# A Macaron block (MoE, state-space mixer, MoE): on GpSimd's queue, the third group's scatter goes ahead of the first group's gather

## The reference

```python
x = L0_attn_x                                    # 4 x 1024 tokens, 256 wide
x = x + 0.5 * ffn(layernorm(x))                  # block 1
x = x + attn(layernorm(x))                       # in_proj, conv, state-space scan, gate, norm, out_proj
x = x + 0.5 * ffn(layernorm(x))                  # block 2, same weights
# ffn: every token goes through 2 shared experts and 4 of 16 routed ones
tidx, tw = _route(x, router_weight, e_bias)      # best 2 of 4 groups, then the 4 best experts
h = silu(x @ gate.T) * (x @ up.T);  y = h @ down.T
routed = sum over the 4 chosen of tw * y;  out = routed + shared
```

## Time and profile before

| what | value |
|---|---|
| time, median of 3 runs | 1771.51 us (1762.28 to 1775.17) |
| the profiled execution's own time | 1766.28 us |
| its span, first to last instruction | 1764.5 us |
| mean granted TensorE clock | 0.911 |
| PE busy | 1460.1 us (83%) |
| DVE, ACT, POOL busy | 1038.3, 702.0, 997.7 us |

### The profile page before, as it was taken

One profiled execution on the slowest core, in us unless ns is written; L12 is line 12 of the kernel. 1 busy time (PEld: TensorE's weight loads), 2 busy tenths in 40 slices (PEclk: granted clock), 3 DMA queues, 4 the chain that ended last, 5 costly groups with the idle time before them and its releaser, 6 DMA issues. The chain is left out here.

```text
span 1764.5 us, 24364 instructions
## 1 busy us (share of the span) xinstructions
PE 1460.1 (83%) x7430; PEld 1218.3 (69%) x7430; DVE 1038.3 (59%) x2279; ACT 702.0 (40%) x1191; POOL 997.7 (57%) x982
## 2 busy tenths in 40 slices
PE   5889989999704689999999998997588989999970
PEld 4678878888603467777777776776577878888860
DVE  5544255335534487888888788886655425533543
ACT  4244434444204444454544444443323433444420
POOL 2706735537464776675767667574170773554746
PEclk9999989999956599999999989999699999999995
DMA  9826456757334000010000100000623645675733
GB/s 377 347 106 229 151 170 219 267 182 261 118 124 139 0 1 12 25 37 13 25 13 24 36 11 25 12 24 12 257 93 106 235 144 172 234 259 179 258 110 122
DMA packets 91286, 226.25 MB, mean 128 GB/s; under 512 B 16673, under 2 KB 29985, under 8 KB 90273
## 3 DMA queue, kind: packets, MB, share of 16 engines
q1 hardware_dynamic: 66592, 157.68, 25.1%
q0 software_dynamic: 24576, 67.14, 11.6%
HBM read 115.72 MB, written 109.05 MB: 127 GB/s over the span
## 5 line engine op out<-in xcount | busy, mean ns | idle before, releaser
L746 PE MATMUL f_gu_ps<-f_wgu,f_xT 128*128 (+1 forms) x1920 | 470.6, 390 | 0.0
L369 POOL DMA_INDIRECT f_gbuf<-yg,f_rows x256 | 261.9, 1023 | 261.0 <-DVE f_xin L617 121.7
L746 PEld LDWEIGHTS f_gu_ps<-f_wgu,f_xT 128*128 128x128 f32 x1920 | 357.5, 196 | 41.1
L345 POOL DMA_INDIRECT xg<-f_xn,f_rows x256 | 251.5, 982 | 210.0 <-DVE f_rows L560 133.9
L596 DVE TENSOR_TENSOR f_h<-f_gu_ps,f_sg 128x256 f32<-128x256 f32 x240 | 101.4, 423 | 349.3 <-ACT f_sg L413 348.3
L767 PE MATMUL f_y_ps<-f_wd,f_hT 128*128 (+1 forms) x960 | 248.1, 387 | 29.1 <-DVE f_hT L602 29.0
L767 PEld LDWEIGHTS f_y_ps<-f_wd,f_hT 128*128 128x128 f32 x960 | 183.0, 193 | 62.2 <-DVE f_hT L602 23.2
L1383 DVE SCALAR_TENSOR_TENSOR at_xs<-at_raw,at_taps,at_xs 128x512 f32<-128x512 f32 x144 | 188.7, 1310 | 29.9 <-POOL at_xs L1122 27.4
L413 ACT ACTIVATE f_sg<-f_gu_ps 128x256 f32<-128x256 f32 x240 | 91.8, 384 | 283.2 <-PE f_gu_ps L746 282.9
L396 ACT COPY f_xT<-f_xT_ps 128x512 f32<-128x512 f32 x224 | 131.4, 587 | 146.0 <-PE f_xT_ps L722 134.9
L617 DVE SCALAR_TENSOR_TENSOR f_xin<-f_gbuf,f_w,f_xin 128x256 f32<-128x256 f32 x256 | 123.7, 485 | 78.6 <-DMA f_gbuf<-yg,f_rows 71.7
(11 more groups left out here) (224 smaller groups left out, 2611.7 us busy)
## 6 DMA issues: line engine op xcount, KB each, us to landing
f_xq<-xg SPq DMA_DIRECT2D x88, 512.0 KB, 4.5
yg<-f_yo SPq DMA_DIRECT2D x176, 256.0 KB, 2.7
xg<-f_gbuf SPq DMA_DIRECT2D x32, 512.0 KB, 17.4
f_wgu<-in_gate_up SPq DMA_DIRECT2D x4, 1280.0 KB, 21.3
at_x_ln<-x SPq DMA_DIRECT2D x10, 512.0 KB, 3.9
f_xin<-in_x SPq DMA_DIRECT2D x8, 512.0 KB, 6.9
xg<-f_xn,f_rows POOLq DMA_INDIRECT x256, 3.7
f_gbuf<-yg,f_rows POOLq DMA_INDIRECT x256, 3.4
```

Source lines behind the costliest of these rows:

```text
L345: G.indirect_dma_start(xg[g], bass.IndirectOffsetOnAxis(ap=rows[g][:, b, k:k + 1], axis=0), xn[:, SUB * TILE0[g] + b, :], None, bounds_che ...
L369: G.indirect_dma_start(gbuf[:, n % GBUF, k, :], None, yg[g], bass.IndirectOffsetOnAxis(ap=rows[g][:, b, k:k + 1], axis=0), bounds_check=2 ...
L746: last = T.matmul(gu_ps[:, j % 2, s * 2 * P:(s + 1) * 2 * P], x_of(k, s, d), weight(wgu[:, :, d, :], experts[s]), start=(d == 0), stop=(d ...
```

## The change

```diff
             rstd_of(t)
         scatter_group(0)
         scatter_group(1)
+        scatter_group(2)
         gather_group(0)
-        scatter_group(2)
         gather_group(1)
         gather_group(2)
```

## The result

The changed kernel took 1846.14 us (median of 4, 1844.93 to 1847.92) against 1773.34 us (median of 4): ratio 1.042, 95% interval 1.0369 to 1.0471. Forecast was 1847 us, slower. The profiled execution took 1847.92 us, and its span is 1846.2 us.

The account below looks back on a forecast made before the run. TensorE (PE) was taken to set the time in the stage touched. Two blocks of 36.0 us stall plus 3.1 restart, no gain, made 78.2 us on 1768.8: 1847 us, range 1832 to 1862.

Parts of the forecast that it names:

- (a): GpSimd's queue, block 1: after waiting 41 us for the addresses, the first moved scatter starts at 262.55 us.
- (b): GpSimd's queue, block 1: 32 scatters at 1.28 us take 41.0 us, so the first gather starts at 303.5.
- Step (c): Group 0's first gather to its combination: 7.24 us (9.23 the upper end), so DVE stands 38.0 us.
- Step (d): PE at L767, block 1: resumes 2.85 us after DVE's combination starts, at 313.6, and loses 36.0 us.
- Step (e): PE's first round after the stall: restart at a lowered clock costs 3.1 us more, making 39.1 a block.
- The sum: Both FFN blocks: 2 x 39.1 = 78.2 us on a mean of 1768.8, giving 1847 us, 4.4% slower.
- rival 2: Third group's start: existing stalls there, 11 us in all, take back part of the loss; 1834 to 1845 us, chance 0.15.
- No gain on the other side: Third group's scatter: its first reader, load L275 at 351.16, has 7 us of spare, so the gain is 0.
- Rival 1: Group 0's gathers land slowly or later combinations wait too: 2 to 9 us more a block, 1851 to 1865, chance 0.15.
- one sign of being wrong: Third group's start: the prediction called itself wrong if the stalls there shrink; no size given.
- Rivals 3 and 4: No change if addresses were ready by 223.7 us (1769 us, chance 0.02); faster through an earlier scatter (1748 us, chance 0.02).
- The rule on the shared port: Moved scatters: would go faster while DVE stands; rule and rows differ by a few tenths of a us a block.

Follow-up runs that it names:

- e1: Kernel before, with GpSimd waiting for the third group's addresses ahead of group 0's gathers, scatters still behind: 1767.85 us, ratio 0.9981.
- e4: Kernel before, with only 16 of the third group's 32 scatters moved ahead of group 0's gathers: 1807.61 us, ratio 1.0198.
- e2: Kernel before, with the new order in the first FFN block alone: 1811.77 us, ratio 1.0224.
- e3: Kernel before, with the third group's scatter placed between group 0's first four and last four gathered blocks: 1800.61 us, ratio 1.0169.
- e9: Changed kernel, with group 0's first combination in event 16 in place of 10: 1811.30 us, ratio 1.0196 to the kernel before.
- e5: Changed kernel, with group 0's combinations from event 22 on in place of 10: 1771.24 us, ratio 0.9971 to the kernel before.
- e6: Kernel before, with the second group's combinations one event (3.25 us) later: 1768.66 us, ratio 0.9957.
- e7: Kernel before, with the second group's combinations two events later, the last ones packed: 1762.38 us, ratio 0.9912.

## Why the prediction was right

**Steps (a) and (b), the date of the first gather.** Forecast 262.55 and 303.5; measured 261.58 and 302.46. Both are 1.0 earlier, because the addresses were: L560 stands at 260.61 in place of 261.58. The second group began no earlier (its first transposition at 225.87, against 225.81), but the granted clock in the 5 us from 225 on was 0.62 in place of 0.50. From that transposition to L560 the eleven kernels take 34.7 to 36.4 us, least where the clock is highest and without regard to GpSimd's order, so nothing puts this 1.0 us down to the change. The 40.9 us between the two dates are as forecast, and 32 scatters at 1.28 us each were the heart of it. e1 and e4 show that this is the right cause: the wait alone costs nothing, and each scatter is worth 1.27 us of DVE's wait.

**Step (c), gather to combination.** Forecast 7.24, measured 6.99 in block 1 and 7.01 in block 2 (1581.49 to 1588.50). The choice of 7.24 over 9.23 was right, but the reason given wasn't: the row called quiet was not. The DMA share from 377.25 to 384.49 was 0.70, against 0.73 in the 9.23 us of block 2, and PE was busy through all of the 7.24. In the stall, at 0.31, the same step took only 0.25 us less. What makes block 2's second group slower (9.23, and 8.55 in the changed kernel) stays open.

**Step (d), PE's loss.** DVE's wait forecast 38.0, measured 37.58 and 37.57; PE resumed 2.85 us after the combination's start in both. PE's 36.0 were 35.48 and 35.47 by its own row.

**Step (e), the restart.** Forecast 3.1, measured 5.93 - 3.25 = 2.68 and 6.39 - 3.25 = 3.14. The other waits of 10.1 us or more, in e2, e3, e4 and e9, were followed by 1.68 to 3.11, so beyond 10 us length adds nothing. Nearly all of it is the clock: by the windows above, PE worked at 0.50 from 312.30 to about 317.6, which is 5.3 us and, by estimate, 2.65 lost. But a short stall doesn't always cost as much as the two of the earlier trace rows. The changed kernel has two at the third group's start in block 1:

```profile
425.06 1.13 PE L767 MATMUL f_y_ps<-f_wd,f_hT 128*128 x4 [2.75 <-DVE f_hT L602]
...
430.63 1.12 PE L767 MATMUL f_y_ps<-f_wd,f_hT 128*128 x4 [2.06 <-DVE f_hT L602]
...
433.97 1.03 PE L767 MATMUL f_y_ps<-f_wd,f_hT 128*128 x4
```

Without the wait inside it, the first of these rounds took 5.57 - 2.06 = 3.51 us and the second 3.34, only 0.26 and 0.09 more than 3.25. The granted clock was 1.00 from 422 to 436 us. In the kernel before, the stall of 2.38 us at the same place cost 2.05 more, and the clock was lower behind it (columns as in rows 2):

```profile
387.00:392.00 5.00, 4.66 (x17) 3.99 (x18) 2.30 (x6) 1.17 (x2) 3.78 (x5) 0.66 0.56 179
```

So the restart is paid where the granted clock has fallen, which it did in every stall of 10 us or more here and only in some of 2 to 3.6 us. (The prediction's 4.7 us at half speed from the earlier trace rows should read 5.1, from 4.19 and 0.9; the sum doesn't use it.)

**The sum.** 39.1 a block was forecast, 37.4 and 37.5 are in the ledger. Of block 1's difference of 1.7, 0.9 is in stall and restart (35.48 + 2.68 = 38.2), 1.0 is the earlier date of step (a), and 0.7 goes the other way at the third group's start; 0.5 is left. In block 2 stall and restart are 38.6, and 1.8 were taken back at the third group's start (see rival 2). The steps held, the stall and its length above all; that the forecast of 1847 met 1846.14 within 1 us was luck: 78.2 was 3 to 5 us too much by the profiles and the medians, and the kernel before is, with more runs, near 1775 and not 1768.8. Its profiled execution (1766.28) was on the low side, which the choice of the mean of four only half made good.

**No gain on the other side.** Confirmed: SyncE's loads of the third group's rows went on in the same rhythm, and e5, where the earlier scatter is free, is not measurably better by its FFN blocks (-0.7 and -1.9 us, where block 2 of e1 and of e2, in the old order, has -4.1 and -1.4).

**The rivals.** Rival 1 (more waits behind the first): the second and later combinations of group 0 wait for nothing, so 6.5 us of time for 5.2 us of gathers was enough. Rival 2 (given back at the third group's start): in block 1 the stalls there were not smaller, PE waited 2.75 and 2.06 us in place of 2.38; in block 2 it waited 2.86 and 1.57 in place of 3.55. With their restarts they cost 5.2 us in place of 4.4 in block 1, and 4.8 in place of 6.6 in block 2. So a give-back of 11 us is refuted, but one sign of being wrong, that the stalls there shrink, did show in block 2, with 1.8 us: the restart was not paid there. Whether the change did that can't be told, for the same stalls vary between kernels that are alike at that place (e1 has 3.46 and 0.93, with 0.26 of restart in the first round). That those stalls are real costs, e6 and e7 show. Rivals 3 and 4 rested on dates that the trace of the kernel before had already excluded.

**The rule on the shared port** (the Trainium skill, "SBUF — State Buffer", section "SBUF: two separate sides") would have GpSimd's DMAs wait while DVE executes an operation in a two-port mode. Whether any DVE operation here runs in one, no run shows. Start to start the moved scatters, 23 of the 32 while DVE waited, took 1.278 us (261.58 to 301.19, 31 steps) against 1.288. The sign agrees; the size is the few tenths of a us in a block that the rows gave.

## What to carry to other kernels

Order two jobs of one in-order queue by the dates of their readers. Here the job whose input comes at 261.8 us and whose reader comes at 351 went ahead of one that was ready at 221 and due at 272.75. The loss can be computed before any run: the time at which the late job is issued behind the other (303.5), plus the 7 us from there to its use, minus the date, minus the 2 us that PE runs ahead, plus one restart. And the date may be the cheaper thing to move: twelve combinations placed up to two events later in DVE's list gave 0.9%, where the order of GpSimd's queue gave nothing that could be measured.

## What I had not expected of the hardware

The stretch between the FFN blocks, which no kernel here touches, took 760 to 774 us in the eleven profiled executions, and most of that spread is on one line, whose gaps add up to 23.1 to 34.3 us. DVE's waits named "issue" (it waited for nothing that the profile shows) at the same instruction, in e6 (760.2 us), the kernel before (760.9), the changed kernel (768.7) and e5 (773.8):

```profile
DVE at_x_res L1397 <- issue: 23.1, 8, 3.6
```
```profile
DVE at_x_res L1397 <- issue: 23.2, 8, 3.6
```
```profile
DVE at_x_res L1397 <- issue: 31.7, 10, 4.1
```
```profile
DVE at_x_res L1397 <- issue: 34.3, 11, 4.1
```

There are 8 such gaps of about 3 us in some executions and 9 to 11 in others: one about every 76 us (704.84, 780.77 and 856.02 us in the changed kernel) and, in some executions, further ones between (970.78, 1128.06). Against the kernel before, the gaps grow by 8.5 us in the changed kernel and by 11.1 in e5, and the stretch by 7.8 and 12.9. What DVE waits for isn't shown: in the program the instruction stands behind two waits, for TensorE's product (`out_in_psum`) and for `res_biased`, and no kernel tried either. For the comparison it means that one profiled execution carries a scatter of some 10 us that is not the change's, and that a difference of spans should be cut by stage before it is explained.
